# The shifted half of the feed-forward input by SBUF-to-SBUF DMAs instead of products with a shift matrix

## What is computed

```python
def shift_token(t):                      # second half of the features comes from the row before
    t1, t2 = jnp.split(t, 2, axis=-1)
    t2 = jnp.pad(t2, ((0, 0), (1, 0), (0, 0)))[:, :-1]
    return jnp.concatenate([t1, t2], axis=-1)
...
x = x + o @ wo                           # end of the attention part: this is x1
h = shift_token(x)                       # the place of the change
mu = h.mean(-1, keepdims=True)
var = h.var(-1, keepdims=True)
h = (h - mu) / jnp.sqrt(var + 1e-05) * lg + lb
h = h @ w1 + b1
a, g = jnp.split(h, 2, axis=-1)
h = a * jax.nn.gelu(g, approximate=False)
x = x + h @ w2 + b2
```

## Time and profile before

| what | value |
|---|---|
| three runs | 847.17, 847.18, 848.62 us, median 847.18 |
| the profiled execution, its own time | 846.62 us |
| its span, first to last instruction | 844.8 us |
| PE busy | 759.1 us, 90% of the span |
| DVE, ACT, POOL busy | 67%, 59%, 52% |
| mean granted TensorE clock | 0.97 |
| DMA queue of SP | 31120 packets, 37.90 MB, 14.0% of 16 DMA engines |

### The profile page before, as it was taken

The page is one execution under the profiler, slowest core; times in us unless marked ns, Lnnn a source line. Parts: engine busy times, 40 slices in busy tenths (PEclk is TensorE's granted clock), DMA queues, the critical chain, the costliest instruction groups (busy, mean ns, idle before and its releaser), DMA issues. The chain is left out here.

```text
span 844.8 us, 17684 instructions
## 1 busy us (share of the span) xinstructions
PE 759.1 (90%) x5088; PEld 652.9 (77%) x5088; DVE 569.6 (67%) x1675; ACT 502.4 (59%) x1241; POOL 441.6 (52%) x625
## 2 busy tenths in 40 slices
PE   5988777989999999999998988999999999999977
PEld 4877655887878787878786877878787878787856
DVE  2798896385858584848485856757575858585842
ACT  2333436366767666666667573757575757575742
POOL 1333464373838383838383645737373737373722
PEclk9999987799999999999999998999999999999999
DMA  7344323151000000000000001010101010101000
GB/s 212 128 137 149 110 57 131 26 219 37 3 29 9 29 8 26 12 20 17 19 18 19 20 2 50 2 51 0 50 0 50 0 50 0 50 0 37 1 26 13
DMA packets 31156, 38.34 MB, mean 45 GB/s; under 512 B 7356, under 2 KB 21776, under 8 KB 31120
## 3 DMA queue, kind: packets, MB, share of 16 engines
q1 hardware_dynamic: 31120, 37.90, 14.0%
HBM read 29.51 MB, written 8.39 MB: 45 GB/s over the span
## 5 line engine op out<-in xcount | busy, mean ns | idle before, releaser
L1351 POOL TENSOR_SCALAR pr<-pr,rl 128x128 f32<-128x128 f32 (+1 forms) x256 | 106.4, 429 | 96.9 <-DVE rl L1129 96.8
L840 ACT ACTIVATE pr<-sm,nb,rn 128x128 f32<-128x128 f32 (+1 forms) x256 | 137.3, 539 | 19.3 <-DVE nb L1124 19.2
L415 PE MATMUL ps<-hT_hi,w_hi 128*128 128x256 f32 (+1 forms) x384 | 110.9, 289 | 1.4 <-DVE hT_lo L1091 1.4
L1120 DVE CUSTOM_DVE_ANT_0 sm<-ps,wmask 128x128 f32<-128x128 f32 (+1 forms) x256 | 81.4, 355 | 41.6 <-PE ps L581 23.0
L415 PE MATMUL ps<-hT_hi,w_lo 128*128 128x256 f32 (+1 forms) x384 | 108.3, 282 | 0.0
L415 PE MATMUL ps<-hT_lo,w_hi 128*128 128x256 f32 (+1 forms) x384 | 107.9, 281 | 0.0
L1314 POOL TENSOR_TENSOR rn<-ss,nhalf 128x16 f32<-128x16 f32 x32 | 95.3, 2978 | 3.7 <-POOL ss L1310 2.0
L798 ACT ACTIVATE sqb<-ps 128x512 f32<-128x512 f32 x64 | 38.2, 598 | 84.9 <-PE ps L415 84.9
L415 PE MATMUL ps<-wqkv_hi,yT_hi 128*128 128x512 f32 x192 | 79.8, 416 | 8.7 <-DVE arena L967 5.3
L1257 POOL TENSOR_SCALAR hrs<-hmv 128x2 f32<-128x2 f32 x16 | 3.1, 193 | 151.7 <-DVE hmv L1145 151.7
L809 ACT ACTIVATE gl<-ps,b_sb 128x256 f32<-128x256 f32 x96 | 45.5, 474 | 53.3 <-PE ps L415 52.9
(11 more groups left out here) (146 smaller groups left out, 2209.2 us busy)
## 6 DMA issues: line engine op xcount, KB each, us to landing
arena<-x SPq DMA_DIRECT2D x16, 256.0 KB, 3.6
ystream<-arena SPq DMA_DIRECT2D x16, 256.0 KB, 2.0
y_next<-ystream SPq DMA_DIRECT2D x16, 256.0 KB, 2.9
y_res<-ystream SPq DMA_DIRECT2D x16, 256.0 KB, 2.6
arena<-L_ffn_w SPq DMA_DIRECT2D x2, 1364.0 KB
arena<-ctx SPq DMA_DIRECT2D x8, 256.0 KB, 4.1
arena<-mask_BxSxS_ik SPq DMA_DIRECT2D x8, 256.0 KB, 2.9
xmid<-arena SPq DMA_DIRECT2D x8, 256.0 KB, 2.0
```

Of the source, the lines that this page charges most:

```text
L415: last = mm(out, lhsT(a), rhs(b), start=(start and i == 0), stop=(stop and i == 2))
L840: A(pr[:, h % NS, a:b], sm[:, h % NS, a:b], ACT.Exp, bias=nb[:, h, t:t + 1], scale=rn8[:, t, h:h + 1], accum_out=ls[:, h, t:t + 1]).then_i ...
L1120: V.tensor_tensor_reduce(sm[:, h % NS, a:b], bank(h % NS)[:, a:b], wmask[:, a:b], 1.0, NEG, ALU.add, ALU.max, mx[:, h, t:t + 1]).then_inc( ...
L1351: G.tensor_scalar(pr[:, h % NS, a:b], pr[:, h % NS, a:b], rl[:, h, t:t + 1], 1.0, ALU.mult, ALU.mult).then_inc(pn_done, 1)
```

## The change

The constant `shift` and the three products with it go. A new SBUF tile `xsh` holds the shifted half of both row tiles. When `x1` is done SP issues two SBUF-to-SBUF DMAs: one moves rows 0 to 126 of both tiles down by one partition (127 partitions, two runs of 128 floats in each), one moves row 127 of tile 0 to row 0 of tile 1. Row 0 of tile 0 is set to zero once. DVE waits for both (`xsh_in`, 32 more per step) instead of for `sh_mm`, and reads `xsh` where it read bank 7. PE's wait that bank 7 is free moves to the transposes. One constant load less, one memset more.

```diff
@@ SP, step
+                if lf is not None:
+                    sp.wait_ge(x1_done, s)
+
+                    sp.dma_start(xsh[1:P, :, :], x1[0:P - 1, :, P:D]).then_inc(xsh_in, 16)
+                    sp.dma_start(xsh[0:1, 1, :], x1[P - 1:P, 0, P:D]).then_inc(xsh_in, 16)
                 if la is not None:
                     wait(sp, x1_done, s)
                     sp.dma_start(flat(y_res), ystream[s]).then_inc(yres_in, 16)
@@ PE, step
-                def shift_rows():
-
-                    pe.wait_ge(x1_done, s)
-                    wait(pe, res_done, f)
-                    o = bank(7)[:, 0:T * P].rearrange("p (t n) -> p t n", t=T)
-                    mm(o[:, 0, :], shift[:, 0:P], x1[:, 0, P:D], start=True, stop=True)
-                    mm(o[:, 1, :], shift[:, 0:P], x1[:, 1, P:D], start=True, stop=False)
-                    mm(o[:, 1, :], shift[:, P:2 * P], x1[:, 0, P:D], start=False, stop=True).then_inc(sh_mm, 1)
...
                 if A:
                     project(0, (0,))
-                if F:
-                    shift_rows()
...
                 if F:
                     pe.wait_ge(hn_done, s)
+                    wait(pe, res_done, f)
                     transpose_rows(hn, 7).then_inc(h_tr, 1)
@@ DVE, step
-                    return (x1[:, t, 0:P], bank(7)[:, t * P:(t + 1) * P])
+                    return (x1[:, t, 0:P], xsh[:, t, :])
 
                 def row_statistics():
-                    dve.wait_ge(sh_mm, s)
+                    dve.wait_ge(x1_done, s)
+                    dve.wait_ge(xsh_in, 32 * s)
@@ POOL, between
                 if b == 1:
+                    G.memset(xsh[0:1, 0, :], 0.0).then_inc(zeros_set, 1)
```

More of the change, by code:

```diff
@@ L50, in build @@
 def build(nc, x, ctx_in, mask, g_xattn, g_ffn, Wq, bq, Wk, bk, Wv, bv, ln_gamma, ln_beta,
-          wqkv, q_scale, k_scale, wo, ln_g, ln_b, w1, b1, w2, b2, rot_tab, win_mask, ident_in, shift_in, out):
+          wqkv, q_scale, k_scale, wo, ln_g, ln_b, w1, b1, w2, b2, rot_tab, win_mask, ident_in, out):
     NB, S, D = x.shape
@@ L87, in build @@
         ident = sb("ident", [P, P])
-        shift = sb("shift", [P, 2 * P])
         wmask = sb("wmask", [P, 3 * P])
@@ L148, in build @@
         x1 = sb("x1", [P, T, D])
+        xsh = sb("xsh", [P, T, P])
         hst = sb("hst", [P, T, 2, 6])
@@ L187, in build @@
              "pT_x", "ctx_mm", "xc_done", "tn_done", "tg_done", "xmid_done", "xrb_done", "y_done_x"))
-        ynext_in, yres_in, xm_in, res_stored = (
-            sem(n) for n in ("ynext_in", "yres_in", "xm_in", "res_stored"))
-        (y_tr, sh_mm, yT_high, yT_done, qk_mm, v_mm2, sq_done, ss_done, ssc_done, rn_done, rn8_done, rot_done, sum_done, ksum_done,
+        ynext_in, yres_in, xm_in, xsh_in, res_stored = (
+            sem(n) for n in ("ynext_in", "yres_in", "xm_in", "xsh_in", "res_stored"))
+        (y_tr, yT_high, yT_done, qk_mm, v_mm2, sq_done, ss_done, ssc_done, rn_done, rn8_done, rot_done, sum_done, ksum_done,
          ks_done, v_done, o_high, hT_high, u_raw, u_high, qk_tr, q_done, k_done, s_mm2, mx_done, nb_done, e_done, rl_done,
@@ L195, in build @@
          hT_done, up_mm, gl_done, u_done, xb_done, dn_mm, yo_done, res_done) = (sem(n) for n in (
-             "y_tr", "sh_mm", "yT_high", "yT_done", "qk_mm", "v_mm2", "sq_done", "ss_done", "ssc_done", "rn_done",
+             "y_tr", "yT_high", "yT_done", "qk_mm", "v_mm2", "sq_done", "ss_done", "ssc_done", "rn_done",
              "rn8_done", "rot_done", "sum_done", "ksum_done", "ks_done", "v_done", "o_high", "hT_high", "u_raw",
@@ L296, in _ @@
                           (qks[:, l, DH:2 * DH], k_scale[l, :].partition_broadcast(P))]
-            small += [(shift[:], shift_in), (wmask[:], win_mask)]
+            small += [(wmask[:], win_mask)]
             for l in range(DEPTH):
@@ L1384, in _ @@
             run_steps(pool, step)
-CONSTS = 16 * 16
-ZEROS = 7
+CONSTS = 16 * 15
+ZEROS = 8
 def host_tables(S):
@@ L1410, in host_tables @@
     return (np.ascontiguousarray(tab, np.float32),
-            np.concatenate([own, prev, own], axis=1).astype(np.float32), np.eye(P, dtype=np.float32),
-            np.eye(P, 2 * P, 1, dtype=np.float32))
+            np.concatenate([own, prev, own], axis=1).astype(np.float32), np.eye(P, dtype=np.float32))
 _INS = ['x', 'ctx_1024', 'mask_BxSxS2_ik1', 'g_xattn', 'g_ffn', 'L0_xattn_Wq', 'L0_xattn_bq', 'L0_xattn_Wk',
@@ L1426 @@
     arrays = {n: np.ascontiguousarray(inputs[n]) for n in _INS}
-    tab, win, eye, down = host_tables(arrays['x'].shape[1])
-    arrays.update(rot_tab=tab, win_mask=win, identity=eye, row_shift=down)
+    tab, win, eye = host_tables(arrays['x'].shape[1])
+    arrays.update(rot_tab=tab, win_mask=win, identity=eye)
     nc = bacc.Bacc("TRN2", target_bir_lowering=False, num_devices=1, dynamic_dma_scratch_size=8192)
```

## The result

The changed kernel takes 1016.93 us (median of 6 runs, 1012.19 to 1017.62), the kernel before 847.00 us (6 runs, 844.56 to 848.62). The ratio is 1.1998, with a 95% interval from 1.1974 to 1.2022: 20% slower. The prediction was 1003 us with a range of 945 to 1085. The direction and the mechanism were right; the forecast is 14 us short. The profiled execution of the changed kernel took 1017.6 us, its span 1015.8 us, against a span of 844.8 before.

What follows compares the result with a forecast made beforehand. PE, or what it waits for, was taken to bound the kernel. Twelve ordinary steps 89, step 1 19.8, steps 8, 9, 16 3.8, 4.5, 7.6, clock 31: 155.7 us on 846.6, forecast 1003 us, range 945 to 1085.

Steps and rivals of the forecast that it cites:

- What bounds the kernel: Serial chain x1, shift, statistics, `hn`, PE: no slack, so later statistics delay PE equally; PE busy 40.17 of 42.45 us.
- One engine for 127 rows: Shift transfer of 127 rows: one DMA engine takes all 254 pieces, landing after 8.6 us; this forecast had 0.80.
- 27.5 ns a piece, 7.0 us for 254: Shift transfer: each 512 B piece takes 27.5 ns, read from the load of `ident`; 254 on one engine take 7.0 us.
- The fixed part: Landing of the shift transfer: 1.6 us besides its pieces, from the `ident` load's 1.8 us less 0.2.
- `hn` 0.13 us sooner: Each step: `hn` reads the shifted half from SBUF in 340 ns, not PSUM in 405; two save 0.13 us.
- The clock, 2.0 us per step: PE at half clock after long waits: 2.0 us lost per step, 1.0 in step 16, 31 us in all.
- upper bound of 3.4 us: Clock loss on PE: at most 3.4 us in each step, adding 22 us to the forecast.
- Step 1, 19.8 us and 2.0 of clock: Step 1: shift transfer queues behind weight loads costing 7.1 us; statistics at 186.95 against 167.07, 19.8 us net, plus clock.
- Steps 8, 9 and 16: Later statistics cost 3.8, 4.5 and 7.6 us net; DVE's weight splits cover part in 8 and 9.
- spread over 16 engines: Rival: 16 engines share the shift transfer, last landing 2.2 us after x1, no clock loss; 24 us, 871 us; chance 0.12.
- A fixed piece cost of 61 ns: Rival: each piece takes 60.8 ns whatever its size, 15.4 us for 254; 1137 us; chance 0.06 with anything over 1085 us.
- Not slower: Rival: both copies land within 1.36 us of x1, 1.2 us after issue, chain starts as before; about 845 us; chance 0.02.

Runs made afterwards that it cites:

- the half transfer: Changed kernel with the 127-row transfer moving tile 0 only, 127 pieces in place of 254, the rest left zero: 959.05 us (one run).
- the kernel of 884.75 us: Changed kernel with the 127 rows cut into 112 and 15, and in step 1 the shift transfers issued ahead of the weight loads: 884.75 us, ratio 1.0455.

## Why the prediction was right, and where it was off

- *What bounds the kernel.* Right. The chain x1, `xsh`, statistics, `hn`, PE has no slack, and its delay was paid in full in the ordinary steps (8.3 us of longer period for 8.5 us of later statistics, with the clock's part taken away). That PE is the engine that waits, and everyone behind it, stands in the two waits of 157 us.
- *One engine for 127 rows.* Right: share 0.07 while they move, and 120 us back when the rows are cut.
- *27.5 ns a piece, 7.0 us for 254.* Right: 27.6 by the half transfer.
- *The fixed part, "so the fixed part is 1.6 us".* This is the term that was too small. Statistics were to start 8.8 us after x1 and start 9.73 after it on average, 9.79 in step 2. SP issues the transfer 0.03 us after x1 and not 0.18. With 7.0 us of pieces, 2.7 us are left where the prediction had 1.6. Of the missing 1.1 us some 0.3 is the one-row copy that lands behind the others (by its removal), which the prediction had left out of this case. The other 0.8 stays open: the 1.6 came from a load out of DRAM, and SP needs 0.76 us to issue the new transfer and not 0.34, but no run shows that the landing counts from the issue's end. Twelve steps of 0.9 us of chain are 11 of the 14 us.
- *`hn` 0.13 us sooner.* It was 0.24: from the start of the statistics to the end of the last `hn` 3.63 us instead of 3.87. The other 0.11 us is the second reduction, which finds its square ready.
- *The clock, 2.0 us per step.* Right: 2.15 measured by keeping PE at work, and 3.9 us at the lower level after the restart in step 2, where the prediction took 4.3. For its upper bound of 3.4 us the prediction gave no row.
- *Step 1, 19.8 us and 2.0 of clock.* 23.8 in place of 21.8, and 15.6 of them from standing behind the weight loads. *Steps 8, 9 and 16*: 6.8, 7.2 and 8.9, forecast 5.8, 6.5 and 8.6. DVE's weight splits did cover part: the wait in step 9 is 5.82 us instead of 9.79. These four are 4 us over in sum, and the first part of the program gave 0.9 back. That the total came within 14 us is not luck: nearly every term was low by a little. Only the first part of the program and `hn` (0.1 us a step) went the other way.
- *The rival "spread over 16 engines", 871 us.* The kernel that does it takes 896.8. It was undersized in the same term: three issues in a row instead of two at 0.34 us, last landing 3.4 us after x1 instead of 2.2, and then clock loss after all, in some steps. *A fixed piece cost of 61 ns* is out. *Not slower* did not come: its condition, a landing 1.2 us after the issue, was met by no copy (the shortest took 1.7 us), and the best version tried, spread, first in its queue and with early statistics, is still 3.2% slower than the three products.

## What to carry to other kernels

Before a computation on a serial chain is replaced by a DMA, compare with the start of whoever waits: here products that were done 1.4 us after their input gave way to a transfer that at its best landed 3.4 us after it, even though it freed the busiest engine. Count the rows of a transfer: 127, a prime number, went to one DMA engine, 124 to four, 126 to about fourteen, and one row split off (126 + 1) gave 120 of the 170 us back. A delay on such a chain also stops TensorE, and can bring a clock loss on top: here 2.15 us on 8.3, and with the short delay of 2.05 us none in some steps and 1.5 in others. And when a transfer moves to another issuer, look at what its old issuer now sends sooner.

## What the runs showed of the hardware beyond that

- With 254 pieces queued on one engine the issuer was held up: SP spent 4.5 to 5.0 us in the issue of the next transfer, whichever that was (11.3 us where the weight loads were queued too). With 127 pieces queued the next issue took 0.94 us.
- Issuing a transfer from SBUF to SBUF took SP 0.67 us with 112 rows, 0.76 with 127, 0.91 with 15 and 0.59 with one; `y_res` takes 0.34, or 0.42 right behind these.
- The one-row copy landed 1.7 us after its issue from SP, with little else moving, and 2.9 us after its issue from ScalarE, with `y_res` moving beside it.
- The loss by the clock comes in steps: in the kernel of 884.75 us, with the same delay, an ordinary step took 44.5 or 46.0 us, and nothing between.
